# An attention and routed-expert layer: the experts' hidden values split from PSUM, and the first expert's weight preparation moved by four tiles

## The reference, cut to what matters

```
xn = layernorm(x)
# causal attention with a linear position bias, scores against xn itself
s  = softmax((xn @ W_qk) @ xn.T / 16 + (kpos - qpos) * slope, causal) @ (xn @ W_v.T)
# routing: each token to its best expert of 8, at most 512 tokens to one expert
p, e = max(softmax(xn @ Wr)), argmax
h  = relu(xe @ W1[e])            # 512 x 256 @ 256 x 1024
ye = (h @ W2[e]) * p             # 512 x 1024 @ 1024 x 256
out = x + s * silu(y)            # y: ye brought back to its tokens
```

## Time and profile before

| | us |
|---|---|
| profiled execution | 486.67 |
| its span | 484.6 |
| median of the runs | 486.47 |
| TensorE matmuls busy | 441.1 (91%) |
| VectorE busy | 343.6 (71%) |
| ScalarE busy | 251.5 (52%) |
| GpSimd busy | 223.0 (46%) |

### The profile page before, as it was taken

How to read it: one execution, slowest core, us unless ns; L and a number is a source line. 1 busy time by engine, 2 the same in 40 slices (tenths; PEclk the granted TensorE clock), 3 DMA queues, 4 the chain that set the end, 5 groups by cost and what they waited for, 6 DMA issues and landing times.

```text
span 484.6 us, 8609 instructions
## 1 busy us (share of the span) xinstructions
PE 441.1 (91%) x3138; PEld 301.9 (62%) x3138; DVE 343.6 (71%) x881; ACT 251.5 (52%) x460; POOL 223.0 (46%) x337
## 2 busy tenths in 40 slices
PE   5777998999999989999999999999999999999960
PEld 2444575666677756767766787666666666666640
DVE  4779587687586757876765653889897979886340
ACT  1443452445544534444434344768686867768630
POOL 4107654333260373822040000257768787878761
PEclk9999998999999999999999999999999999999995
DMA  6982812603500485124002405347759475753140
GB/s 217 345 317 79 217 58 66 208 1 90 173 1 1 122 312 158 64 71 150 2 21 70 82 12 216 89 160 168 208 163 236 123 252 151 224 105 92 49 130 32
DMA packets 64313, 63.43 MB, mean 131 GB/s; under 512 B 36902, under 2 KB 58156, under 8 KB 62224
## 3 DMA queue, kind: packets, MB, share of 16 engines
q1 hardware_dynamic: 53472, 40.78, 29.4%
q0 software_dynamic: 5632, 16.73, 11.1%
q10 hardware_dynamic: 5168, 5.37, 3.4%
HBM read 30.29 MB, written 25.43 MB: 115 GB/s over the span
## 4 chain that ended last, share of the span: by engine, by line
PE 50%; DVE 29%; ACT 8%; issue 5%; POOL 3%; DMA 2%; SPq 1%; DVEq 0%; POOLq 0%; ACTq 0%
PE bank L1123 11%; PE bank L1125 11%; PE bank L1124 11%; DVE pmax L840 6%; DVE w_l L866 5%; PE bank L1194 4%; PE bank L1209 4%; PE bank L1212 4%; PE bank L1211 4%; DVE hid_l L884 3%; DVE sc L807 2%; DVE pT_l L823 2%; ACT hid_h L1049 1%; ACT sc L1026 1%; DMA sc<-in_w_r 1%
## 5 line engine op out<-in xcount | busy, mean ns | idle before, releaser
L1032 ACT ACTIVATE pT_h<-bank 128x512 f16<-128x512 f32 (+2 forms) x80 | 42.3, 530 | 82.9 <-PE bank L1194 82.7
L823 DVE SCALAR_TENSOR_TENSOR pT_l<-bank,pT_h 128x512 f16<-128x512 f32 (+2 forms) x80 | 48.6, 608 | 42.9 <-ACT pT_h L1032 41.6
L1209 PE MATMUL bank<-v_h,pT_h 128*128 128x257 f16 x272 | 75.0, 276 | 0.6 <-DVE pT_l L823 0.6
L1212 PE MATMUL bank<-v_h,pT_l 128*128 128x257 f16 x272 | 74.3, 273 | 0.0
L1211 PE MATMUL bank<-v_l,pT_h 128*128 128x256 f16 x272 | 74.0, 272 | 0.0
L1123 PE MATMUL bank<-w_h,hid_h 128*128 128x256 f16 x256 | 69.8, 273 | 2.7 <-DVE w_l L866 2.6
L884 DVE TENSOR_TENSOR hid_l<-hid,hid_h 128x512 f16<-128x512 f32 x64 | 49.6, 781 | 30.3 <-ACT hid_h L1049 30.1
L1125 PE MATMUL bank<-w_h,hid_l 128*128 128x256 f16 x256 | 69.8, 273 | 0.0
L1124 PE MATMUL bank<-w_l,hid_h 128*128 128x256 f16 x256 | 69.8, 273 | 0.0
L1123 PE MATMUL bank<-xT,qT_h 128*128 128x512 f16 (+3 forms) x160 | 56.0, 353 | 7.3 <-DVE cmin L807 5.8
L1026 ACT ACTIVATE sc<-sc,rmin 128x512 f32<-128x512 f32 (+2 forms) x72 | 43.3, 659 | 30.2 <-DVE rmin L814 30.2
(11 more groups left out here) (169 smaller groups left out, 953.4 us busy)
## 6 DMA issues: line engine op xcount, KB each, us to landing
raw<-in_w_e SPq DMA_DIRECT2D x5, 2048.0 KB, 9.1
sc<-in_w_e SPq DMA_DIRECT2D x3, 2048.0 KB, 7.6
slots<-empty ACTq DMA_DIRECT2D x1, 4224.0 KB, 26.1
out<-xg SPq DMA_DIRECT2D x8, 512.0 KB, 3.3
rows<-xg SPq DMA_DIRECT2D x8, 512.0 KB, 4.2
rows<-so SPq DMA_DIRECT2D x8, 512.0 KB, 3.0
xg<-in_x SPq DMA_DIRECT2D x6, 512.0 KB, 4.3
xg<-in_x ACTq DMA_DIRECT2D x2, 512.0 KB, 6.0
```

The costliest lines, as they stand in the source:

```text
L823: v.scalar_tensor_tensor(pT_l[:, t % 2, cols], tr_ps[n % 2][:, 0:w], P_UP, pT_h[:, t % 2, cols], ALU.mult, ALU.subtract).then_inc(pT_lo, 1)
L1209: pe.matmul(pv_ps[t % 2][:, 0:D + 1], pT_h[:, t % 2, rows_], v_h[:, at, q, 0:D + 1], start=kb == 0, stop=False)
L1212: last = pe.matmul(pv_ps[t % 2][:, 0:D + 1], pT_l[:, t % 2, rows_], v_h[:, at, q, 0:D + 1], start=False, stop=kb == t % NT)
```

## The change

- The splits of the hidden values: ScalarE makes `hid_h` in f16 straight from PSUM with ReLU, and VectorE makes `hid_l` as max(PSUM, 0) - `hid_h` straight from PSUM. `hid`, the scale in between and the semaphore `h_read` go. up(f+2) waits for `hid_l` of block f.
- To make that possible the powers of two differ: the tokens are scaled by 4 in place of 1024, expert weights have 4 bits of reach above their maximum's power in place of 14 (`E_TOP`), and the result's factor `ymul` follows. Instructions and sizes stay the same there.
- The first expert's maxima move from tiles 4 to 7 to tiles 8 to 11, its scale from tile 8 to 12, its splits from tiles 8 to 15 to tiles 12 to 19; SP's load of the second expert's weights moves from tile 16 to 20. The second expert's maxima stay.

```diff
-X_UP = 2.0 ** 10
-ACC_DOWN = 2.0 ** -18
+X_UP = 2.0 ** 2
+ACC_DOWN = 2.0 ** -8 / X_UP
+E_TOP = 4
...
-        FIRST_MAX, FIRST_SCALE, FIRST_SPLIT = (4, 5, 6, 7), 8, tuple(range(8, 16))
+        FIRST_MAX, FIRST_SCALE, FIRST_SPLIT = (8, 9, 10, 11), 12, tuple(range(12, 20))
+        SECOND_LOAD = 20
...
-                if t == NT:
+                if t == SECOND_LOAD:
 
                     sp.wait_ge(w_lo, 2 * PIECES)
                     sp.dma_start(raw[:, :, :], w_k[1]).then_inc(w_in[1], 16)
...
-            def scales(top, exp, up, dn):
+            def scales(top, exp, up, dn, bits=W_TOP):
...
-                    scales(w_back, wexp[:, :], wup[k][:, :], wdn[:, :])
-                v.tensor_scalar(ymul[k][:, :], wdn[:, 0:1], wdn[:, 1:2], UNDO, ALU.mult, ALU.mult
+                    scales(w_back, wexp[:, :], wup[k][:, :], wdn[:, :], E_TOP)
+                v.tensor_scalar(ymul[k][:, :], wdn[:, 0:1], wdn[:, 1:2], 1.0 / X_UP, ALU.mult, ALU.mult
...
                 dve.wait_ge(h_hi, m + 1)
-                v.tensor_tensor(hid_l[:, f % HB, :], hid[:, f % 2, :], hid_h[:, f % HB, :], ALU.subtract
-                                ).then_inc(h_lo, 1)
+                v.scalar_tensor_tensor(hid_l[:, f % HB, :], sc_ps[f % 2][:, :], 0.0, hid_h[:, f % HB, :],
+                                       ALU.max, ALU.subtract).then_inc(h_lo, 1)
...
-            def hidden(m, f, first=False):
+            def hidden(m, f):
 
                 act.wait_ge(h_full, m + 1)
-                if not first:
-
-                    act.wait_ge(h_lo, m - 1)
-                a_.activation(hid[:, f % 2, :], sc_ps[f % 2][:, :], ACT.Relu, scale=ACC_DOWN).then_inc(h_read, 1)
-                act.wait_ge(h_read, m + 1)
-                a_.activation(hid_h[:, f % HB, :], hid[:, f % 2, :], ACT.Copy).then_inc(h_hi, 1)
+                a_.activation(hid_h[:, f % HB, :], sc_ps[f % 2][:, :], ACT.Relu).then_inc(h_hi, 1)
...
                 if not first:
 
-                    pe.wait_ge(h_read, e * NF + f - 1)
+                    pe.wait_ge(h_lo, e * NF + f - 1)
```

More of the change, by code:

```diff
@@ L204, in layer_kernel @@
         put_idx = [sb(f"put_idx{k}", [P, SJ], U32) for k in range(2)]
-        hid = sb("hid", [P, 2, CAP])
         hid_h = sb("hid_h", [P, HB, CAP], F16)
@@ L292, in layer_kernel @@
         h_full = sem("h_full")
-        h_read = sem("h_read")
         h_hi = sem("h_hi")
@@ L712, in _ @@
                             ).then_inc(small_maxed, 1)
-            def scales(top, exp, up, dn):
+            def scales(top, exp, up, dn, bits=W_TOP):
                 step(v.tensor_scalar(exp, top, 2.0 ** -100, None, ALU.max))
                 step(v.tensor_scalar(exp.bitcast(I32), exp.bitcast(I32), 0x7F800000, None, ALU.bitwise_and))
-                step(v.tensor_scalar(up.bitcast(I32), exp.bitcast(I32), float((2 * 127 + W_TOP) << 23), -1.0,
+                step(v.tensor_scalar(up.bitcast(I32), exp.bitcast(I32), float((2 * 127 + bits) << 23), -1.0,
                                      ALU.subtract, ALU.mult))
-                step(v.tensor_scalar(dn.bitcast(I32), exp.bitcast(I32), float(W_TOP << 23), None, ALU.subtract))
+                step(v.tensor_scalar(dn.bitcast(I32), exp.bitcast(I32), float(bits << 23), None, ALU.subtract))
             norm_stats(1, range(GT))
@@ L855, in scale @@
                     step(v.tensor_reduce(wtop[:, :], wall[:, :].rearrange("p (q m) -> p m q", m=2), AX.X, ALU.max))
-                    scales(wtop[:, :], wexp[:, :], wup[k][:, :], wdn[:, :])
+                    scales(wtop[:, :], wexp[:, :], wup[k][:, :], wdn[:, :], E_TOP)
                 else:
                     dve.wait_ge(w_told, e - 1)
-                    scales(w_back, wexp[:, :], wup[k][:, :], wdn[:, :])
-                v.tensor_scalar(ymul[k][:, :], wdn[:, 0:1], wdn[:, 1:2], UNDO, ALU.mult, ALU.mult
+                    scales(w_back, wexp[:, :], wup[k][:, :], wdn[:, :], E_TOP)
+                v.tensor_scalar(ymul[k][:, :], wdn[:, 0:1], wdn[:, 1:2], 1.0 / X_UP, ALU.mult, ALU.mult
                                 ).then_inc(w_scaled, 1)
@@ L1095, in _ @@
             for f in range(LEAD):
-                hidden(f, f, True)
+                hidden(f, f)
             def expert(e):
```

## The result

The changed kernel takes 490.67 us (median of 8 runs, 488.49 to 491.41), the kernel before 486.54 (8 runs, 485.67 to 489.58): a ratio of 1.0062, 95% interval 1.0033 to 1.009. Forecast were 480.9 and a range of 479.3 to 483.6. The kernel became slower. The profiled execution took 489.56, its span is 487.8 (484.6 before).

What follows compares the result with a forecast made beforehand. TensorE is nearly always busy, so only its pauses pay: experts -3.6, maxima -1.6, clock -1.7, scale 0, splits +1.3, together -5.6 us from 486.47, giving 480.9; range 479.3 to 483.6.

Steps and rivals of the forecast that it cites:

- One instruction of ScalarE, one of VectorE: Hidden split: one ScalarE instruction of 0.59 us replaces two; VectorE's `hid_l` from PSUM takes 0.69, without long values.
- VectorE's list starts earlier: Expert boundary: scale step 0.46 us earlier, a 0.34 wait gone, so VectorE's list starts 0.80 earlier.
- All boundary pauses go, the bank's return costs nothing: Expert stage: TensorE's five boundary pauses vanish, 3.36 us, and up blocks don't wait for the bank, 0.
- the last block's 0.28: Last down pair of the expert stage: with `hid_l` earlier, TensorE's wait shrinks by 0.28 us.
- Maxima, scale, splits: Attention stage: moved maxima save 1.6 us, moved scale 0, splits of tiles 17 and 18 cost 1.3.
- The clock: Attention stage after 77.66: shorter pauses keep the clock from falling, 1.7 us saved; rival that a drop stays or comes, 0.21.
- The bank is given back later: Expert stage: up(f+2) waits for VectorE's `hid_l`, not ScalarE's read; it ends 0.21 us before needed, so cost 0.
- I put this wait at 0: Expert stage: the up block's wait for VectorE's `hid_l` to free its bank was taken as 0 us.
- All five boundary pauses go: 3.36 us: Expert boundaries: VectorE's earlier list removes all five TensorE pauses, with about 0.1 us to spare.
- up blocks that wait for `hid_l`: Expert stage: waits of TensorE's up blocks for VectorE's `hid_l` were named as a sign the forecast is wrong.
- a VectorE that isn't earlier (0.59): Expert stage: without VectorE's earlier list, TensorE would lose 0.59 us at the up block, then that much less at the boundary.

Runs made afterwards that it cites:

- e5: The changed kernel, unedited, run again on chip 14: 480.13 us, ratio 0.9883 to the kernel before.
- e1: The kernel before with only the moved maxima, scale, splits and second load, old hidden split kept, on chip 8: 484.05 us, ratio 0.9971.
- e2: The changed kernel with the old tiles for maxima, scale, splits and second load, so only the new split from PSUM, on chip 8: 481.32 us, ratio 0.9907.
- e7: The changed kernel with one GpSimd memset ahead of the very first row fetch, none in the experts, on chip 14: 480.59 us.
- e8: The changed kernel with a third PSUM bank for up blocks and the first expert's splits in tiles 12 to 15, two pairs per tile, on chip 14: 482.97 us.
- e12: The changed kernel with one GpSimd memset between the puts and the row fetches of each expert, on chip 9: 480.50 us, ratio 0.9864.
- e13: The changed kernel with a GpSimd memset ahead of each row fetch of the experts, on chip 9: 481.12 us, ratio 0.9877.
- the halves on chip 8: The kernel before with the moved tiles only, 484.05 us, and the changed kernel with the old tiles, 481.32 us.
- e18: The kernel before with only the moved maxima, scale, splits and second load, on chip 6: 486.37 us, ratio 0.9982.
- e9: The changed kernel, unedited, run a third time, on chip 11: 490.04 us, ratio 1.0039 to the kernel before.
- e16: The changed kernel with a GpSimd memset ahead of the four puts of each expert, on chip 6: 490.50 us, ratio 1.0058.

## Why the prediction was wrong

Term by term, first what held, by the first trace, e5 and e1:

- *One instruction of ScalarE, one of VectorE.* `hid_h` 597 ns in the median (0.59 taken). `hid_l` has no long values: 683 with a maximum of 693 after, where e1, with the old split, still has 1221. The rows (tile view: count: shortest/median/longest ns), of after and of e1:

```profile
L884 DVE SCALAR_TENSOR_TENSOR hid_l<-bank,hid_h x64: 673/683/693, 290.9 to 468.3; 128x512 f16<-128x512 f32 x64
```
```profile
L885 DVE TENSOR_TENSOR hid_l<-hid,hid_h x64: 677/693/1221, 291.5 to 463.2; 128x512 f16<-128x512 f32 x64
```

- *VectorE's list starts earlier.* The scale step stands 0.26 behind the transpose where it stood at 0.72: 0.46 earlier, as worked out. The wait of 0.34 one block on is gone too.

```profile
322.21 0.22 PE L1312 MATMUL bank<-ident,wrep 2*128 2x2 f32 x1
```
```profile
322.47 0.16 DVE L716 TENSOR_SCALAR wexp<-bank 128x2 f32<-128x2 f32 x1
```

- *All boundary pauses go, the bank's return costs nothing.* This holds where there are no late starts: 21.20 us per expert in e2, e5, e7, e8, e12 and e13, among others, and the last block's 0.28 came as well (from the last `wrep` transpose to the last matmul 33.93 in e5, 34.21 before). It is the floor: 96 matmuls of 0.109 and 48 of 0.215 are 20.8, and the transposes come on top.
- *Maxima, scale, splits.* TensorE's waits in the attention stage, first trace:

```profile
75.66 0.39 PE L1118 MATMUL bank<-xT,qT_h 128*128 128x512 f16 x1 [0.52 <-DVE cmin L807]
...
134.47 0.39 PE L1118 MATMUL bank<-xT,qT_h 128*128 128x512 f16 x1 [0.56 <-DVE cmin L807]
...
182.22 0.18 PE L1156 MATMUL bank<-chosen,before 128*128 128x32 f16 x1 [1.07 <-DVE chosen L795]
...
183.82 0.39 PE L1118 MATMUL bank<-xT,qT_h 128*128 128x512 f16 x1 [0.90 <-DVE cmin L807]
```

Against the earlier trace rows: 1.94 near 77 are 0.52; the pair of 0.57 and 0.50 behind tile 8 is one of 0.56 behind tile 12; 0.41 and 0.24 are 1.07 and 0.90, each 0.66 more, to the hundredth what was taken for the splits of tiles 17 and 18. e1 has the same waits; e5, which had half clock just ahead of it, has one of 0.65 instead of the two.
- *The clock.* This term is not shown. The first trace has no drop behind 76, where 0.53 stood, but e2, with the maxima in their old tiles and waits of 1.09 and 0.87 at 75.45 and 76.82, has none there either. The first trace, then e2:

```profile
76.00:79.60 3.60, 3.60 (x27) 2.39 (x25) 1.96 (x9) 2.17 (x4) 2.14 (x9) 1.00 0.54 109
469.00:472.40 3.40, 3.31 (x16) 2.38 (x17) 1.22 (x4) 0.84 (x2) 0.00 (x0) 0.51 0.00 0
```
```profile
76.80:80.40 3.60, 3.58 (x25) 2.47 (x26) 3.50 (x10) 1.89 (x4) 2.06 (x10) 1.00 0.35 73
```

So no run shows that the moved maxima are worth the 1.7 us. The clock fell elsewhere: in the first trace it is 0.50 from 45.7 to 52.5, twice as long as before (46.9 to 50.3), and 0.51 behind the wait of 2.58 near the end. In e5 it is 0.65 from 177.4 to 180.9 (1.2 us of work lost), behind a wait of 2.43; the same wait in the first trace, 2.42 at 176.54, preceded no drop. (The prediction's "1.94 of some 3 us" are 1.94 of 2.45, from 75.21 to 77.66.)

On chip 14 all this adds up to -5.3 us (485.42 to 480.13), where -5.6 was forecast; the halves on chip 8 give -1.4 and -4.1. That it comes so near is in part luck, since 1.7 of the 5.6 was the clock.

**The step that failed** is "*The bank is given back later*", where the prediction says "I put this wait at 0", and with it "All five boundary pauses go: 3.36 us" and the 0.28 us of the last block. They take for granted that ScalarE learns of a full bank when TensorE's last matmul ends; by the prediction's sum 0.21 us were to spare at the tightest block. On the chip of the first trace it learns of one bank per expert 2.3 to 3.3 us later. In the expert shown the up block's wait for `hid_l` then costs 0.77 us (0.88 from 357.45 to 358.33 where 0.11 is normal) in place of 0, and the boundary keeps 0.42 (0.64 from 362.14 to 362.78 where 0.22 is normal) of its 0.65. The stage pays 1.0 to 1.4 us per expert over 21.20, 6.1 in the five windows, and at the end 4.3 more: from the last `wrep` transpose to its last matmul TensorE takes 38.25 us there and 33.93 in e5, which is the wait of 2.58 and 1.7 of half clock. Together 10.4, less 0.2 by which e5 enters the experts later and 0.9 that the last puts give back: the 9.2 between the spans (487.8 and 478.6). The prediction named the right sign of being wrong, "up blocks that wait for `hid_l`", but priced it only for a VectorE that isn't earlier (0.59) and gave it no chance.

**What I could have seen.** No row of the trace before shows a late start, and nothing in it prices one; that a chip would answer so could not be read from it. What could be read was how thin the margin is, 0.21 us at the tightest block between VectorE's `hid_l` and the up block that now waits for it, where the kernel before needed only ScalarE's read. The other thing is what happens to GpSimd. I used its contention with VectorE in one direction only. The trace before has two fetches of 1.5 us, one beside a `w_l` (357.57), one beside a `hid_l` (359.43), both with two inputs in SBUF; the changed kernel has 0.95 at both. The Trainium skill, page "SBUF — State Buffer", section "Who interferes with whom", says that a DMA that seems stalled by a VectorE instruction is one for which GpSimd makes the descriptors, and lacks port time to do it. The rows fit that, but they don't show that the new `hid_l` is what made the fetches shorter: `w_l` stands beside them after the change as well, only at another moment (353.90 beside the fetch of 353.46). The range had no case for "something next to this gets faster and hurts", and 0.92 for faster was too sure for that.

**Not settled.** Why TensorE's signal comes late, and why on chips 11, 9 and 6 and not on 8 and 14. That the row of GpSimd's DMAs sets it off is shown in one direction: a gap of 1.8 us in the row, or one ahead of each fetch, takes the late starts away on chip 9 (480.50 and 481.12 beside 491.99). That the change made them by closing the row up is not shown, for e18 has them beside stretched DMAs. Nor is it the length of the row: rows of 10.0 to 11.8 us without a gap have late starts, and e12's of 11.7 with a gap has none. It isn't the loading of code, as far as the packets tell: in the second trace with late starts (e9) no packet of the instruction queues falls into five of the seven gaps. It isn't slower transfers: the 4096-byte packets of GpSimd's queue take 0.25 us in the mean from 353.8 to 357.0 in the first trace and 0.24 in the same stretch of e5. Open is also why the kernel before itself takes 485.4 on two chips and 487.5 to 488.1 on three; its one trace comes from a chip of the first kind, by its landing times (below), and says nothing on the second.

## What to carry to other kernels

When a change hands a buffer back later, work out how late a signal in that loop may come before TensorE stands still: here one that came 3.1 us late cost 1.2 us per expert, where the old order took late signals of up to 2.3 us at next to no cost. Look at what the neighbours do as well: long rows of indirect DMAs can be broken with other work of the same engine where there is room, and 1.8 us between four and four were worth 11.5. Read a late start back to the event that released it before it is put down to the engine that starts late. And before a slower time is put down to the code, run the same code on another chip: here the sign of the change depends on it, and a comparison is worth something only beside a control on the same chip.

## What the runs showed of the hardware

- The semaphore event of a TensorE matmul can come up to 4.8 us behind the matmul's end (3.1 in the expert shown of the first trace, 4.8 in e16, 0.01 to 0.02 on chips 8 and 14), mostly at the same block, while GpSimd issues indirect DMAs in a row without a gap. ScalarE, which waits for it, starts 0.02 us behind the event, and at some of these places TensorE stops in the middle of a block. All profiles of the changed kernel on chips 11, 9 and 6 have it, and the old experts on chip 6; none on chips 8 and 14. Two forms of spacing took it away (e12, e13).
- The profiles of these chips differ also where there is no late start. Of the landing times of the puts and of the `xT` transposes at least one is missing in every profile taken on chips 11, 9 and 6, and none on chips 8 and 14. Whether the missing records and the late events have one cause is not shown. DMA issues of the first trace, then of e5 (what, count, median us to landing):

```profile
out<-xg,put_idx POOLq DMA_INDIRECT x16
```
```profile
out<-xg,put_idx POOLq DMA_INDIRECT x16, 2.6
```

- The trace of before that the prediction rests on has those times (2.5 and 2.7), the trace of after hasn't: by this mark the two were taken on different kinds of chip. The kernel before, run beside the changed one, had a median of 487.80 (5 runs), against 486.47 alone (3 runs).
